# One core of Trainium2: a state space stage rewritten as interleaved streams, with 32x32 tiles for its small levels and the first expert layer's gathers inside it

## The reference, cut to what matters

```python
x = x + 0.5 * _L0_ffn_ref(_layernorm(x, axis=-1), ...)
x = x + _L0_attn_ref(_layernorm(x, axis=-1), ...)
x = x + 0.5 * _L0_ffn_ref(_layernorm(x, axis=-1), ...)
x = x + 0.5 * _L1_ffn_ref(_layernorm(x, axis=-1), ...)
x = x + _L1_attn_ref(_layernorm(x, axis=-1), ...)
x = x + 0.5 * _L1_ffn_ref(_layernorm(x, axis=-1), ...)
```

```python
proj = x @ W_in
...
Cr = _rope(Cm, cos[:, :, None, :], sin[:, :, None, :])
Br = _rope(Bm, cos[:, :, None, None, :], sin[:, :, None, None, :])
...
xg = (lam * dt)[..., None, None] * xh
xb = ((1.0 - lam) * dt * alpha)[..., None, None] * x_prev
...
dmat = jnp.exp(jnp.where(mask[None, None, :, :, None], diff, NEG))
sg = jnp.einsum('bclgn,bcmgrn->bclmgr', Cc, Bgc) * SCALE
...
y_intra = jnp.einsum('bclmgr,bclmge,bcmgerp->bclgep', sg, dg, xgc) + ...
S = cd[..., None, None] * S + s
y_inter = SCALE * jnp.einsum('bclgn,bclge,bcgenp->bclgep', Cc, dec_in, Sprev)
y = _rms(y * jax.nn.silu(z))
return y @ W_out
```

## Time and profile before

| what | us |
|---|---|
| median of 3 runs (lowest to highest) | 1775.69 (1751.07 to 1775.83) |
| the profiled execution, its own time | 1772.93 |
| its span, first to last instruction | 1771.1 |
| first expert layer | 0 to 227 |
| gathers of its combined rows | 227 to 309 |
| state space stage, with the clearing ahead | 309 to 998 |
| second expert layer | 998 to 1200 |
| last three layers | 1200 to 1771 |

### The profile page before, as it was taken

One profiled execution on the slowest core, in us unless ns is written; L12 is line 12 of the kernel. 1 busy time (PEld: TensorE's weight loads), 2 busy tenths in 40 slices (PEclk: granted clock), 3 DMA queues, 4 the chain that ended last, 5 costly groups with the idle time before them and its releaser, 6 DMA issues. The chain is left out here.

```text
span 1771.1 us, 28517 instructions
## 1 busy us (share of the span) xinstructions
PE 1194.0 (67%) x8800; PEld 811.3 (46%) x8800; DVE 1205.5 (68%) x2660; ACT 717.0 (40%) x1216; POOL 650.7 (37%) x787
## 2 busy tenths in 40 slices
PE   4279900438855866586478547992589888889894
PEld 4169900226523643364256426982444444444332
DVE  7979934286737754774668487984677787786653
ACT  2458800320131013111301206871178677768782
POOL 0456467015511640273136106645433244140100
PEclk9999955668976887698769658995689899999996
DMA  7035411100000000000000312340000000000000
GB/s 208 0 84 162 81 51 50 42 1 1 1 1 0 0 1 0 0 0 1 0 0 0 123 56 67 92 80 24 12 13 5 16 13 19 7 15 11 2 13 6
DMA packets 57418, 55.70 MB, mean 31 GB/s; under 512 B 11355, under 2 KB 45957, under 8 KB 57285
## 3 DMA queue, kind: packets, MB, share of 16 engines
q1 hardware_dynamic: 48196, 35.43, 6.6%
q0 software_dynamic: 9088, 18.63, 4.9%
HBM read 33.30 MB, written 20.73 MB: 31 GB/s over the span
## 5 line engine op out<-in xcount | busy, mean ns | idle before, releaser
L1814 ACT ACTIVATE l_probs<-l_ps 128x1024 f32<-128x1024 f32 (+1 forms) x320 | 287.9, 946 | 109.6 <-PE l_ps L1700 107.7
L709 POOL DMA_INDIRECT ffn_yg<-y_rows,ffn_index x156 | 155.9, 999 | 162.9 <-POOLq L470 96.9
L1206 PE MATMUL ssm_ps<-ssm_X,ssm_SM 128*128 128x256 f32 x768 | 201.4, 426 | 9.0 <-DVE ssm_Y L1351 9.0
L1719 PE MATMUL l_ps<-l_probs,l_vs 128*32 128x512 f32 (+3 forms) x1536 | 165.9, 521 | 30.0 <-DVE l_oTs L2046 16.2
L1206 PEld LDWEIGHTS ssm_ps<-ssm_X,ssm_SM 128*128 128x128 f32 x768 | 162.9, 216 | 39.9 <-issue 12.1
L792 ACT ACTIVATE ffn_hT<-ffn_ps_h,experts_b1T,experts_scales 128x256 f32<-128x256 f32 x312 | 150.8, 563 | 25.4 <-PE ffn_ps_h L739 24.4
L256 POOL DMA_INDIRECT combine_og<-o_rows,combine_place x128 | 127.4, 995 | 55.4 <-issue 36.1
L1018 POOL TENSOR_TENSOR ssm_X<-ssm_zx,ssm_xw 128x1024 f32<-128x1024 f32 x32 | 68.3, 2140 | 201.7 <-PE ssm_ps L1211 135.0
L1091 ACT COPY ssm_bct<-ssm_ps 64x384 f32<-64x384 f32 x32 | 15.1, 472 | 310.8 <-PE ssm_ps L1159 310.8
L2037 DVE TENSOR_TENSOR l_probs<-l_probs,last_tri 128x256 f32<-128x256 f32 x256 | 102.2, 437 | 39.3 <-ACT l_probs L1814 37.9
L1700 PE MATMUL l_ps<-l_qkT 32*128 32x512 f16 (+3 forms) x768 | 110.2, 339 | 18.3 <-ACT l_probs L1814 16.1
(11 more groups left out here) (314 smaller groups left out, 2818.6 us busy)
## 6 DMA issues: line engine op xcount, KB each, us to landing
o_rows<-ffn_out_sb SPq DMA_DIRECT2D x78, 128.0 KB, 1.9
y_rows<-ffn_y SPq DMA_DIRECT2D x8, 512.0 KB, 3.0
kept_w<-experts_w SPq DMA_DIRECT2D x16, 256.0 KB
experts_w<-kept_w SPq DMA_DIRECT2D x16, 256.0 KB, 5.4
ffn_yg<-y_rows,ffn_index POOLq DMA_INDIRECT x156
x_res<-in_L_attn_x SPq DMA_DIRECT2D x4, 512.0 KB, 6.3
prep_raw<-in_L_ffn_W SPq DMA_DIRECT2D x1, 2048.0 KB, 10.7
prep_raw<-in_L_ffn_W SPq DMA_DIRECT2D x8, 256.0 KB, 6.4
```

Of the source, the lines that this page charges most:

```text
L709: g_.indirect_dma_start(yg[:, i % RING, j].rearrange("p n d -> p (n d)"), None, w.y_rows.ap(), bass.IndirectOffsetOnAxis(ap=index[:, n:n + ...
L1206: t_.matmul(ps_o[:, o * DI:(o + 1) * DI], SM[:, i % 2, k, r, :], xr(i, k, r), start=(k != 1 and r == 0), stop=(k != 0 and r == 1), skip_gr ...
L1719: ins = t_.matmul(ps_o[VP * h:VP * h + VP, q0 % H:q0 % H + width], vs[:, s % 2, kb, h, :], probs[:, n % PSLOTS, i, at:at + width], start=( ...
L1814: s_.activation(probs[:, w % PSLOTS, i:i + n, 0:width], ps_s[w % 2][:, i:i + n, 0:width], ACT.Exp, scale=SCALE / (UNIT * UNIT)).then_inc(S ...
```

## The change

**1. Gathers.** The block at L849 goes. What both expert layers share (`o_rows`, semaphores, kept weights) moves into a class `ExpertRows`, so that `Combine` can outlive the first expert stage, and its place and gates with it. `core.clear` now stands ahead of the gathers. The state space program itself fetches, adds and counts in groups of 4 tiles (`GROUP`), on a semaphore of the combine.

**2. One program.** The loops over batches go. The whole stage is one block, written out for 32 tiles. Each job is a stream with times at which its pieces are due, and `interleave` sorts the pieces of all streams on each engine. Tile n has its levels at `K[n] = 105 + 12 n`; a group's gathers, norm, transposing and raw projection stand at `G_AT`, a batch's coefficients at `C_AT`, the wide projections with Silu at `X_AT`. These are units of the table; the engines run by semaphores in the resulting order. Batch b+1's jobs stand beside batch b's chunks, and `zx`, `outp`, `xw` and `rot` have 12 slots instead of 8. PSUM: three banks for the outputs, one for dots, and a ring of 4 for everything else.

**3. Levels.** The masks are 128x4x32 instead of 128x6x128. Leaf, strict leaf, level 8 and level 16 are 32x32 tiles on the diagonal, four to a level and rank. Level 32 is two tiles of 32x32, level 64 one of 64x64. These two need no mask and come from the dots by a copy on ACT. With the one that brings the state in, these are 39 products of 256 columns in place of 13. The dots are cut in the same way (14 in place of 2 per chunk, the two ranks on partitions 0 to 63 and 64 to 127). B of both ranks and C lie on all 128 partitions, and the state of both ranks is stacked likewise: one product of 128 rows brings it in.

**4. Moves between engines.** The square of `raw` and the copies out of PSUM into `raw` go from DVE to ACT. The layer norm goes from DVE and ACT to POOL, in nine small steps per group with a root by `pow`. Scaling and adding are cut to three pieces of 128x512, so that a pair of sums is left for POOL instead of three.

The diff, cut to its core:

```diff
-        if layer == 0:
-            with nc.Block() as block:
-                @block.gpsimd
-                def _(pool):
-                    for tile in range(TILES):
-                        combine.fetch(pool, tile)
-
-                @block.vector
-                def _(dve):
-                    for tile in range(TILES):
-                        combine.add(dve, tile)
         core.clear()
...
+        PERIOD = 12
+        FIRST = 105
+        K = [FIRST + PERIOD * n for n in range(TILES)]
...
+                def near_level(n, o, k, x, r, start, stop):
+                    for m in range(0, P, BLOCK):
+                        rows = slice(m, m + BLOCK)
+                        ins = t_.matmul(o[rows], near[rows, n % 2, k, r, :], weighed(n, x, r, rows), start=start, stop=stop,
+                                        skip_group_check=True)
+                    return ins
...
-                        for k in range(6):
-                            o = 0 if k < 2 else k - 1
-                            for r in range(R):
-
-                                t_.matmul(ps_o[:, o * DI:(o + 1) * DI], SM[:, i % 2, k, r, :], xr(i, k, r),
-                                          start=(k != 1 and r == 0), stop=(k != 0 and r == 1), skip_group_check=True)
+                    for k in range(2):
+                        for r in range(R):
+                            near_level(n, ps_o[0][:, 0:DI], k, k, r, k == 0 and r == 0, k == 1 and r == 1)
+                    for r in range(R):
+                        near_level(n, ps_o[1][:, 0:DI], 2, 3, r, r == 0, r == 1)
+                        ins = t_.matmul(ps_o[0][64:128, DI:], far[0:64, n % 2, r, 32:96], weighed(n, 2, r, slice(0, 64)),
+                                        start=(r == 0), stop=(r == 1), skip_group_check=True)
...
+                def fetch(g):
+                    for j in range(GROUP):
+                        yield 2.6 * j
+                        combine.fetch(pool, g * GROUP + j)
...
+                def norm(g):
+                    yield 17
+                    pool.wait_ge(combine.counted, (g + 1) * GROUP)
...
+                def scale(n):
+                    for i in range(3):
+                        yield (4.3, 6.2, 7.2)[i]
+                        dve.wait_ge(S["o_done"], 3 * n + i + 1)
+                        if n:
+                            dve.wait_ge(S["partial"], n)
+                        v.tensor_tensor(Y6[:, 2 * i:2 * i + 2].rearrange("p k (h d) -> p (k h) d", h=H),
+                                        ps_o[i].rearrange("p (q d) -> p q d", d=PD),
+                                        outp[:, n % SLOTS, 2 * i:2 * i + 2, :].rearrange("p k h -> p (k h)").unsqueeze(2)
+                                        .broadcast_to([P, 2 * H, PD]), ALU.mult).then_inc(S["scaled"], 1)
```

1095 lines of the change are left out of this document (624 added, 471 removed).

## The result

The changed kernel takes 1537.41 us (median of 4 runs, 1535.42 to 1540.59), the kernel before beside it 1763.44 us (4 runs, 1751.07 to 1775.83). The profiled execution spans 1533.6 us, 237.5 less than before. The executions of the kernel before take either about 1751 or about 1776 us and the profiled one (1772.93) is of the longer kind, so up to 22 of these 237.5 us may be that difference and not the change, and no trace shows where it lies; the medians differ by 226.0.

The account below looks back on a forecast made before the run. No engine was full: PE and DVE waited in turn, with gathers and a serial chain to overlap. Filling, 24 tiles at 16 us and seven at 10.9 end the stage at 793 against 998.5, giving 1565 us, range 1500 to 1640.

Parts of the forecast that it names:

- Start and filling: State space stage: gathers start at 234.7 us after the clearing; filling and the chain put tile 0's levels at about 315.
- the way out and the clearing: End of the stage: last tile's way out 14 us and clearing 4.3, as before, so the stage ends at 793.
- 24 tiles at 16 us: Tiles beside which the next batch is prepared: DVE's 12.8 + 0.6 us at 0.83 give 16 each, ending at 699.
- a share taken from another program: DVE's share of 0.83 in the first 24 tiles, from the last layer's interleaved streams, busiest engine at 0.8 to 0.87.
- term for the two engines' meetings: DVE and POOL hold each other up: about 1 us per tile added, 0.6 in the sum.
- 1 us named for semaphore gaps: Per tile of the stage: 1 us added for gaps at semaphores.
- Seven tiles at 10.9: Last seven tiles, only chunks left: DVE 8.1, PE 10, a tile 10.2 to 11.7 before; 10.9 each, ending at 775.
- Tiles side by side: PE's four 32x32 diagonal tiles run at once, 5.9 us of levels and state per tile; rival in turn: 1853 us, 0.06.
- price that I put on turns: Rival of diagonal tiles in turn: 39 products at 0.45 us, 17.6 per tile on PE; chance 0.06.
- The gathers wait for DVE: Rival: POOL's gathers take 3 us each instead of 1.0 while DVE holds the port, 1640 us; 0.22 together with half clock.
- Nothing hidden: Rival: fixed stream order lets a late wait stop all, only the removed gather part is left, 1700 us; chance 0.05.
- What would show it: Profile signs: PE idle some 25 us, first L1190 near 315, DVE near 410 us busy, clock above 0.9 from 320.

Follow-up runs that it names:

- runs with four and six sets: Changed kernel with x weighed by four or six sets on DVE instead of five, the rest on POOL: 1575.77 and 1573.94 us; tiles 0 to 31 take 434.9 and 431.3.
- run one by one: Changed kernel with the first 20 small products of a tile issued diagonal block by diagonal block instead of level by level: 1715.8 us, one run.
- gathers in front: Changed kernel with all 32 tiles' gathers and additions put back in a block ahead of the stage: 1573.92 us.
- batch after batch: Changed kernel with its table stretched so a batch's gathers, projections and coefficients stand behind the last chunk of the batch before: 1667.65 us.

## Why the prediction was right, point by point

**Start and filling: 315 forecast, 309.2 measured.** The gathers began at 230.9 instead of 234.7, and from there to the levels of tile 0 it took 78.3 us where the sum has 79. This is 6 of the 30 us that the stage ended earlier than my 793 (762.6). The 24 tiles are 12 more, the last seven 17; the way out and the clearing took 22 us where I had 18.

**24 tiles at 16 us: right, 15.5 measured** ((690.33 - 318.42) / 24). The terms held: DVE 13.0 us per tile (311.2 of 370 us, times 15.5) against 13.4 (12.8 of work and 0.6 for meetings), at a share of 0.84 against 0.83, PE 12.8 against 13.1, POOL 9.6 against 10.2. What the sum did not say is that the tiles take from 7.9 to 20.3 us. The mean hides parts with different bounds. That a share taken from another program gave the right mean for all of them is in part luck. The runs with four and six sets show that a bound read off the mean share (DVE at 0.84) is not a bound. The term for the two engines' meetings (named as 1 us, used as 0.6) stands for a real mechanism, which works on POOL more than on DVE. The 1 us named for semaphore gaps is in the sum only by way of the share.

**Seven tiles at 10.9: wrong in size, 8.5 measured.** This is the larger miss, 17 us. My own sum for PE there was 10.1, and I took the row of the old chunks (10.2 to 11.7) instead, in which neither engine was full (PE 9.0 and DVE 8.5 of 10.2 us); that their hand-written order bound them is my reading, and no run tested it. PE's terms, from the rows above: levels and state in 5.55 us (5.9 forecast), dots 1.14 (1.8), the rest 2.06 (2.4).

**Tiles side by side: right.** The Trainium skill's rule (TensorEngine Tiling, Gotcha 1), that different row tiles can't use one PSUM bank at a time, gives turns and a slower kernel. The trace does not bear it out for four 32x32 tiles on the diagonal that write one bank at different partitions: 40 passes in 2.29 us. The order of the queue decides, as the run one by one shows. The price that I put on turns, 0.45 us a product, was too high at full clock (0.3) and too low at half clock (0.5: ten passes, five products, in 2.62 us).

**The gathers wait for DVE: a small part of it happened.** Their mean is 1.13 us against 0.94 in front, the longest 3.66; the case of 3 us each did not come. Four of the 64 took 3.0 to 3.7 us. Each of the four met one of DVE's weighings and ended 0.8 to 0.9 us behind its end; one of them, with the weighing:

```profile
445.92 2.97 POOL L260 DMA_INDIRECT combine_og<-o_rows,combine_place  x1 [0.30 <-issue]
445.24 2.81 DVE L1558 TENSOR_TENSOR ssm_X<-ssm_zx,ssm_xw 128x2560 f32<-128x2560 f32 x1
```

What the gathers cost was POOL's time and the landing behind it, 26 us of pace, of which moving them in POOL's order gave 20 back. This the prediction had named (38 us of POOL work in two or three tiles) but not priced.

**Nothing hidden: this case did not come.** The overlap is worth 88.6 us, the gathers' place 36.5, and the small tiles, which are no part of this case, 24.

**What would show it:** PE's standstill (23 us), the first near level and the mean of the gathers came as said. DVE was busy 422 us in the stage where I said 410, and the clock was 0.88 from 320 to 690 where I said above 0.9. The tiles of the last batch took less than the 12 us that would have meant an error.

**Where the 236 us lie.** The table and two runs give a split. On the way to tile 0 the change gained 90.5 us; with the gathers in front 74.6 of them are lost again. In the pace it gained 146.1; batch after batch loses 88.6 of them again, and 57.5 are left. These are inside the batches: the 28 distances there add up to 236.7 us in that run, where the kernel before has 303.2, while the three stretches between batches, now with gathers in them, take 283.4 against 274.4. So a lighter tile gives some 66 us. Of what made it lighter only the small tiles were undone (26 us of distance, in the overlapped program); how the rest divides between the dots, the scaling and the moves of single instructions to ACT and POOL stays open.

## What to carry to other kernels

When two serial parts are laid beside each other, make the sum per engine for each part of the new period and not for its mean: a mean share of 0.84 on one engine hid three bounds in turn, and moving 16 gathers by three tiles gained 20 us, where moving 512 columns of work from one engine to another gained nothing. Price the stretches without overlap by the new sum and not by the old rows, if no engine was full in these. Small matrix tiles gained here only because neighbours in the queue use different places of the array.

## What was not expected of the hardware

- Products of 32x32 on six different places (four on the diagonal, two beside it) run side by side: 24 passes of 256 columns in 1.01 us, where 24 of 128x128 took 5.45.
- On one place alone a pass of 256 columns follows the last by 0.13 us at full clock (ten in 1.32 us), faster than the 0.23 of a pass of 128x128 or of a group of four places.
- PE can be busy 96% of the time and still be granted 0.65: with 20 of a tile's small products on one place at a time (76.7 of 80 us, one run), while the same products side by side kept 1.00 (58.2 of 59.6 us).
- Changing between 32x32 and 64x64 places costs some 0.14 us, an estimate (two changes less gave 0.27 a tile), though the weight loads show 0.4 us of idle time at each.
- An addition of 0.72 us on POOL takes 3.24 when it meets DVE's weighing of 2.82 us, in 16 of the 32 tiles. Busy time on POOL is therefore no measure of its work, and with four sets DVE's is none either.
- A gather that meets such a weighing waits for its end too (2.97 us instead of 0.94), but only 4 of 64 did.
